# Two-layer attention and mixture-of-experts kernel: expert stages flat over all tiles, routing weights by DMA instead of by matmul

## The chip, the cores and the metric

The kernel runs on one core of one Trainium2 chip. The metric is the device time of one execution in microseconds (us), lower is better; a kernel's time is the median of its runs. A profiled execution also leaves a trace of every instruction.

## The reference, cut to what matters

Two layers run over 2048 tokens of width 128 (two sequences of 1024). Each layer is normalise, attention, gate, experts, and adds its result to the tokens. Layer 0 has 32 experts of inner width 64 and a shared one of 128; layer 1 has 16 experts of inner width 176 and a shared one of 352. Each token uses 4 experts, with weights from the gate; all experts are computed for all tokens, and the weight is zero where an expert was not chosen.

```python
cw = jnp.zeros((T, E), xf.dtype).at[jnp.arange(T)[:, None], indices].add(weights)
def body(y, p):
    w1e, b1e, w3e, b3e, w2e, b2e, we = p
    h = jax.nn.silu(xf @ w1e + b1e) * (xf @ w3e + b3e)
    return (y + we[:, None] * (h @ w2e + b2e), None)
y, _ = jax.lax.scan(body, y0, (w1, b1, w3, b3, w2, b2, cw.T))
z = jax.nn.silu(xf @ sw1 + sb1) * (xf @ sw3 + sb3) @ sw2 + sb2
return (y + z).reshape(shape)
```

Layer 1 has no biases, and the output projection of its attention is added to the same sum.

## The kernel before

**Stages.** `two_layers` runs six blocks one after the other: `prepare`, attention and `experts` for layer 0 (k = 0), then the same three for layer 1 (k = 1).
**Routing weights.** At the end of an attention stage the gate's result `cw` [tokens, experts + 1] is transposed by TensorE (`weights_turned`, L192) into PSUM, ScalarE copies the high part (float32r) to rows 0.. of `cw_split` (`weights_hi`, L203), and VectorE writes the rest to rows 64.. (`weights_lo`, L211).

**Experts.** All experts of a layer lie side by side as hidden rows, cut in chunks of 128 rows: K = 17 chunks for layer 0 and K = 25 for layer 1 (the last has 96 rows). Tokens are cut in NC = 4 tiles of 512. Every factor of a product is split in a high and a low part, so a product is three float32r matmuls. For one chunk and one tile:

- TensorE `rise(c)`: three matmuls for g (L1165 to L1167), three for u (L1169 to L1171), one (L1172) that spreads the routing weights over the chunk's rows: the 0/1 matrix `sel` times `cw_split` into a PSUM bank `c_ps`. 
- ScalarE: gate = silu(g) (L1226), later hid_hi = rounded hid (L1232).
- VectorE: up = u * gate (L1296 with bias for k = 0, L1298 for k = 1), hid = c_ps * up (L1302).
- GpSimd: hid_lo = hid - hid_hi (L1251).
- TensorE `fall(c)`: waits for hid_hi and hid_lo, then three matmuls into the one bank `y_ps` (L1179 to L1181), which sums over the chunks of the tile.

Each of these matmuls has 512 columns, 10 in a chunk. TensorE's order in a tile is rise(0), rise(1), rise(2), fall(0), rise(3), fall(1) and so on, then fall(K-2), fall(K-1). The token tile is the body of a hardware loop (`Fori`) on every engine, so rise(0) of a tile comes after the last fall of the one before, and `y_ps` is free only when VectorE has copied it to `yT` (L1314 for k = 0, L1316 for k = 1). g, u and c_ps have two banks each, y one, and one (z) serves the end. For k = 0 two matmuls (L1193, L1194) start y with the b2 bias; for k = 1 three more per tile add the projection (L1185 to L1187), whose input VectorE normalises inside the tile, at chunks K-6 to K-3 (L1286 reciprocal, then L1287 to L1289).

**Weights.** Sync (SP) loads w1, w3, w2 and `sel` in groups of up to three chunks into a ring of two (L1110, L1113); ScalarE copies the high parts (`split_hi`, L1214, `sel` too), GpSimd writes the low parts (`split_lo`, L1146). Groups 0 and 1 are split ahead of the first tile; groups 2 and 3 ahead of the first two gates, and later ones at chunks 3, 6, 9 and so on of the first tile. From the second tile on there are no weight loads.

**Transposes.** `yT` is [features, tokens]. For k = 0 it is turned back to rows at the start of `prepare` of layer 1 (L292, L377), for k = 1 at the end of `experts` (L1207, L1322), all 16 blocks after the last tile, followed by the store of the output (L1126).

## Time and profile before

| | us |
|---|---|
| median of 3 runs | 1406.43 (1398.53 to 1409.87) |
| the profiled execution's own time | 1408.63 |
| its span, first to last instruction | 1406.8 |
| TensorE busy | 1181.4 (84%) |
| ScalarE, VectorE, GpSimd busy | 761.5, 719.5, 550.8 |

The span begins with `prepare` and the first attention (to 235 us); experts of layer 0 run from 236 to 444 us, the second `prepare` and attention from 444 to 1115, experts of layer 1 from 1115 to the end. In a timeline a row is one instruction: start, length, engine, line, operands, and in brackets how long its engine sat idle before it and who released it. Matmuls are pipelined: successive starts tell their pace, and the lengths overlap.

### The profile page before, as it was taken

What the parts mean: (1) busy time and instruction counts of PE and PEld (TensorE: products, weight loads), DVE (VectorE), ACT (ScalarE), POOL (GpSimd) and SP (SyncE); (2) the same over time, 40 slices, a digit from 0 to 9 for tenths busy, and PEclk for the clock granted to TensorE, in tenths of its full rate; (3) what the DMA queues carried; (4) which work ended last, traced back from release to release, by engine and by line L of the source; (5) the groups of instructions that cost most, each with busy time, mean ns of one, the idle gap of its engine ahead of it and who ended that gap; (6) DMA issues with size and microseconds to landing.
All of it is one profiled execution on the core that took longest, in us unless ns stands there. A gap on an engine that the chain in (4) does not pass through costs nothing. (4 is left out here: it accounts for less than half of the span.)

```text
span 1406.8 us, 23122 instructions
## 1 busy us (share of the span) xinstructions
PE 1181.4 (84%) x8332; PEld 727.0 (52%) x8332; DVE 719.5 (51%) x998; ACT 761.5 (54%) x1136; POOL 550.8 (39%) x725
## 2 busy tenths in 40 slices
PE   3599996789986622899999999999999378898897
PEld 3233332567764521455555555555554256677685
DVE  5122221345556520676666666666664036575656
ACT  1388885644442101475777777777775255344443
POOL 1255553745443010033333333333322367454554
PEclk9999998899997555597999999999999689999999
DMA  3311101300000273877788888788761241000001
GB/s 114 149 43 49 42 31 60 105 0 0 0 0 6 82 253 111 270 188 206 185 222 227 215 235 226 223 222 224 225 206 28 81 142 29 0 0 0 0 0 30
DMA packets 119933, 155.76 MB, mean 111 GB/s; under 512 B 27806, under 2 KB 110880, under 8 KB 119840
## 3 DMA queue, kind: packets, MB, share of 16 engines
q1 hardware_dynamic: 101280, 145.30, 33.1%
q0 software_dynamic: 18560, 9.23, 4.4%
q8 instruction: 57, 0.93, 0.3%
q14 instruction: 36, 0.29, 0.1%
HBM read 81.97 MB, written 72.34 MB: 110 GB/s over the span
## 5 line engine op out<-in xcount | busy, mean ns | idle before, releaser
L1009 DVE TENSOR_REDUCE a_part<-a_duo 128x2 f32<-128x1024 f32 x256 | 311.5, 1225 | 196.3 <-PE a_duo L873 195.0
L971 ACT ACTIVATE a_probs<-a_duo 128x1024 f32<-128x1024 f32 x256 | 261.8, 1023 | 105.1 <-PE a_duo L912 99.0
L1251 POOL TENSOR_TENSOR f_hid_lo<-f_hid,f_hid_hi 128x512 fp32r<-128x512 f32 (+1 forms) x168 | 216.8, 1292 | 202.3 <-ACT f_hid_hi L1232 202.3
L818 POOL DMA_DIRECT2D scr_y1c<-a_y x256 | 132.0, 524 | 320.8 <-DVE a_y L1000 319.6
L967 ACT ACTIVATE a_rel<-a_rel_ps 128x384 f32<-128x384 f32 x256 | 126.0, 492 | 135.4 <-PE a_rel_ps L855 114.8
L623 ACT ACTIVATE a_probs<-a_duo 128x1024 f32<-128x1024 f32 x192 | 147.8, 813 | 36.0 <-PE a_duo L581 34.5
L927 PE MATMUL a_acc_ps<-a_probs,a_v 128*32 128x256 f32 x2048 | 166.9, 398 | 0.3 <-issue 0.2
L855 PE MATMUL a_rel_ps<-a_emb_all,a_q 24*128 24x384 f32 x256 | 121.0, 473 | 53.8 <-DMA a_kb<-scr_kb 31.0
L855 PEld LDWEIGHTS a_rel_ps<-a_emb_all,a_q 24*128 24x128 f32 x256 | 50.2, 196 | 161.6 <-issue 97.5
L570 POOL TENSOR_TENSOR a_probs<-a_probs,const 128x256 f32<-128x256 f32 x128 | 95.2, 763 | 86.7 <-ACT a_probs L623 86.7
L1226 ACT ACTIVATE f_gate<-f_g 128x512 f32<-128x512 f32 (+1 forms) x100 | 59.7, 597 | 121.0 <-PE f_g L1167 120.8
L1302 DVE TENSOR_TENSOR f_hid<-f_c,f_up 128x512 f32<-128x512 f32 (+1 forms) x168 | 116.1, 691 | 8.5 <-POOL f_hid_lo L1251 2.9
L1298 DVE TENSOR_TENSOR f_up<-f_u,f_gate 128x512 f32<-128x512 f32 (+1 forms) x100 | 68.8, 688 | 100.8 <-PE f_c L1172 84.1
L1232 ACT ACTIVATE f_hid_hi<-f_hid 128x512 fp32r<-128x512 f32 (+1 forms) x168 | 104.7, 623 | 24.5 <-DVE f_hid L1302 24.5
L601 PE MATMUL a_acc<-a_probs,a_v 128*32 128x256 f32 (+1 forms) x1280 | 116.3, 379 | 0.1
L912 PE MATMUL a_duo<-const,a_rel_raw 128*128 128x128 f32 x704 | 114.5, 290 | 0.0
L900 PE MATMUL a_duo<-a_q,a_ka 25*128 25x512 f32 (+3 forms) x416 | 104.0, 404 | 2.0 <-DMA a_q<-a_rows 0.7
L1165 PE MATMUL f_g<-x_hi,f_w_hi 128*128 (+1 forms) x168 | 69.4, 413 | 37.7 <-ACTq L1236 21.1
L581 PE MATMUL a_duo<-a_q,a_k 24*128 24x512 f32 (+3 forms) x384 | 86.3, 449 | 16.4 <-DMA a_k<-scr_k 15.1
L873 PE MATMUL a_duo<-a_ka,a_q 24*128 24x512 f32 (+3 forms) x416 | 99.1, 444 | 0.7 <-DVE a_rows L1020 0.7
L1179 PE MATMUL f_y<-f_hid_hi,f_w_hi 128*128 128x512 f32 (+1 forms) x168 | 69.7, 415 | 33.9 <-POOL f_hid_lo L1251 33.9
L912 PEld LDWEIGHTS a_duo<-const,a_rel_raw 128*128 128x128 f32 x704 | 75.8, 143 | 36.9 <-issue 30.5
(199 smaller groups left out, 2032.8 us busy)
## 6 DMA issues: line engine op xcount, KB each, us to landing
scr_rel<-a_rel SPq DMA_DIRECT2D x128, 384.0 KB, 3.9
a_rel_raw<-scr_rel SPq DMA_DIRECT2D x128, 384.0 KB, 4.3
f_raw<-in_w SPq DMA_DIRECT2D x33, 192.0 KB, 2.7
scr_q<-q_hi SPq DMA_DIRECT2D x4, 1024.0 KB, 7.9
scr_y1c<-a_y POOLq DMA_DIRECT2D x256, 8.0 KB, 3.4
a_q<-scr_q SPq DMA_DIRECT2D x40, 96.0 KB
a_k<-scr_k SPq DMA_DIRECT2D x32, 96.0 KB
a_q<-scr_q POOLq DMA_DIRECT2D x24, 96.0 KB, 5.4
```

The lines of the kernel that those rows point to most:

```text
L601: ins = pe.matmul(acc[h % 2][to:to + 32, lo:QUARTER], vs[:, pair % 2, hd, kt, :], probs[:, n % KEPT, hd, c * QUARTER + lo:(c + 1) * QUARTE ...
L623: act.activation(probs[:, n % KEPT, :, lo:HALF], duo[n % 3][:, :, lo:HALF], ACT.Sigmoid, scale=SCALE).then_inc(sig_done, 1)
L818: pool.dma_start(scr["y1c"][w, b, head, :, at:at + QUARTER], ys[32 * (2 * hd + c) + HD * w:32 * (2 * hd + c) + HD * (w + 1), h % 2, :]).th ...
L855: pe.matmul(rel_ps[:, 0:BAND], qs[to, home(pair), j * P:(j + 1) * P], emb_all[to, :], start=True, stop=True).then_inc(rel_ready, 1)
L912: ins = pe.matmul(out[:, at:at + P], rel_raw[:, (8 * pair + j) % RING, hd, c:c + P], ident, is_transpose=True, start=False, stop=True, ski ...
L927: ins = pe.matmul(acc[to:to + 32, 0:QUARTER], vs[:, pair % 2, hd, kt, :], probs[:, n % 4, at:at + QUARTER], start=(n % 8 == 0), stop=(n % ...
L967: act.activation(rel_sb[:, e % 4, r % 2, :], rel_ps[:, 0:BAND], ACT.Copy).then_inc(saved_act, 1)
L971: act.activation(probs[:, n % 4, :], bank_pair("t", n)[:], ACT.Exp, scale=SCALE).then_inc(exp_done, 1)
L1009: dve.tensor_reduce(part[:, h % 2, x, :, j % 4], bank_pair("s", m)[:].rearrange("p (h t) -> p h t", h=2), AX.X, ALU.max, negate=True).then ...
L1232: act.activation(hid_hi[0:m, c_ % 4, :], hid[0:m, c_ % 2, :], ACT.Copy).then_inc(hi_ready, 1)
L1251: pool.tensor_tensor(hid_lo[0:m, c % 4, :], hid[0:m, c % 2, :], f32(hid_hi[0:m, c % 4, :]), ALU.subtract).then_inc(lo_ready, 1)
L1302: dve.tensor_tensor(hid[0:m, c % 2, :], w, up[0:m, c % 2, :], ALU.mult).then_inc(hid_ready, 1)
```

## The change

1. *Routing weights by DMA.* `cw_split`, `sel`, its loads and copies, and the matmul L1172 go. ScalarE copies the transposed weights to one tile `cwT`; SP stores it to HBM (`scr["cw"]`) at the end of the attention stage and waits for the landing. In the expert stage SP reads, for each chunk and tile, the row of each expert that owns hidden rows of the chunk, broadcast over those partitions, into `share`, a ring of WB = 4. A chunk has one or two owners: 33 such DMAs per tile for k = 0 and 39 for k = 1, 288 in all, of 256 KB per chunk. `share_out(n)` waits for `hid_ready` n - 3.
2. *u in place.* u has three banks; VectorE writes up over u in PSUM, and hid = u * share.
3. *Flat.* One unrolled sequence over n = tile * K + chunk, 68 and 100 chunks, on every engine; no loop. rise(n) comes before fall(n-2) across tiles too. y has two banks. VectorE takes y of a tile out at chunk 3 of the next (`finish`).
4. *fall* waits for hid_hi, issues its first two matmuls, and only then waits for hid_lo.
5. *Turn inside.* TensorE transposes a finished tile at chunk 5 of the next into z, VectorE adds it to x at chunk 7 (`residual`), in both layers; `prepare` of layer 1 loses its transposes. The last tile is turned at the end of the stage.
6. *Bias.* b2 isn't split any more: one plain float32 matmul per tile, `b2` times `cwT`, ahead of the tile's first fall.
7. SP's order: loads 0 and 1, shares 0 to 3, the attention result (1 MB for k = 0, moved from ahead of the loads; 2 MB for k = 1), then in chunk order the other loads (each waits for `raw_lo`) and shares. The layer 1 normalisation of the projection's input moves from chunks K-6.. to K-8...

```diff
+def weights_stored(router, sb, scr, sp):
+    sp.wait_ge(router.cw_saved, NC)
+    sp.dma_start(scr["cw"][0:E + 1, :], sb["cwT"][0:E + 1, :]).then_inc(router.cw_stored, 16)
+    sp.wait_ge(router.cw_stored, 16)
...
 # SP
+            def share_out(n):
+                ti, c = n // K, n % K
+                wait(sp, hid_ready, n - WB + 1)
+                for e, a, b in owners(c):
+                    row = scr["cw"][e:e + 1, ti * CH:(ti + 1) * CH]
+                    sp.dma_start(share[a:b, n % WB, :], bass.AP(row.tensor, row.offset, [[0, b - a], [1, CH]])).then_inc(share_loaded[n % WB], 16)
...
+            for n in range(WB):
+                share_out(n)
...
+            for n in range(M):
+                if n in starts[:-3]:
+                    load(starts.index(n) + 2)
+                if n >= WB:
+                    share_out(n)
...
 # TensorE
-                    pe.wait_ge(gate_ready, ti * K + max(c - 1, 0) + 1)
-                    pe.wait_ge(hid_ready, ti * K + max(c - 1, 0) + 1)
-                    pe.matmul(w, sel[:, ch], sb["cw_split"][:, cols], start=True, stop=True).then_inc(u_ready, 1)
+                wait(pe, gate_ready, n - 1)
+                wait(pe, hid_ready, n - 2)
...
+                if c == 0:
+                    wait(pe, y_ready, ti - 1)
+                    if k == 0:
+                        pe.matmul(y, b2[0:E + 1, :], sb["cwT"][0:E + 1, cols], start=True, stop=False)
+                pe.wait_ge(hi_ready, n + 1)
+                pe.matmul(y, w_hi[2][0:m, ch], hid_hi[0:m, n % 4, :], start=(k == 1 and c == 0), stop=False)
+                pe.matmul(y, w_lo[2][0:m, ch], hid_hi[0:m, n % 4, :], start=False, stop=False)
+                pe.wait_ge(lo_ready, n + 1)
+                ins = pe.matmul(y, w_hi[2][0:m, ch], hid_lo[0:m, n % 4, :], start=False, stop=(k == 0 and c == K - 1))
...
+            for n in range(M + 2):
+                if n < M:
+                    rise(n)
+                if n >= 2:
+                    fall(n - 2)
+                if n >= K + 5 and n < M and (n - 5) % K == 0:
+                    turn((n - 5) // K - 1)
+            turn(NC - 1)
...
 # VectorE
+            for n in range(M):
+                dve.wait_ge(u_ready, n + 1)
+                dve.wait_ge(gate_ready, n + 1)
...
+                    dve.tensor_tensor(u, u, g, ALU.mult).then_inc(up_ready, 1)
+                dve.wait_ge(share_loaded[n % WB], 16 * shares(n))
+                wait(dve, lo_ready, n - 1)
+                dve.wait_ge(up_ready, n + 1)
+                dve.tensor_tensor(hid[0:m, n % 2, :], u, w, ALU.mult).then_inc(hid_ready, 1)
+                if k == 1 and K - 8 <= c < K - 4:
+                    quotient(ti, c - (K - 8))
+                if ti and c == 3:
+                    finish(ti - 1)
+                if ti and c == 7:
+                    residual(ti - 1)
+            finish(NC - 1)
+            residual(NC - 1)
```

## Rows read from the trace of the kernel before

**Rows 1.** Stretches: length; PE, PEld, DVE, ACT, POOL busy; clock, DMA share, GB/s.

```profile
1122.00:1142.00 20.00, 14.49 (x33) 9.78 (x34) 4.18 (x7) 11.16 (x24) 10.44 (x12) 0.60 0.62 214
...
1345.00:1385.00 40.00, 40.00 (x178) 33.12 (x177) 25.43 (x35) 19.51 (x36) 22.87 (x18) 1.00 0.00 0
```

**Rows 2.** Timeline of one steady chunk, experts of layer 1, first tile.

```profile
1185.79 0.39 PE L1172 MATMUL f_c<-cw_split,f_sel 128*128 x1
...
1188.07 0.62 ACT L1232 ACTIVATE f_hid_hi<-f_hid 128x512 fp32r<-128x512 f32 x1
1188.29 0.39 PE L1179 MATMUL f_y<-f_hid_hi,f_w_hi 128*128 128x512 f32 x1
...
1188.77 1.29 POOL L1251 TENSOR_TENSOR f_hid_lo<-f_hid,f_hid_hi 128x512 fp32r<-128x512 f32 x1 [0.86 <-ACT f_hid_hi L1232]
...
1190.55 0.39 PE L1179 MATMUL f_y<-f_hid_hi,f_w_hi 128*128 128x512 f32 x1
```

**Rows 3.** Timeline of the end of that tile: reciprocal, last chunks, next tile's start.

```profile
1187.64 3.34 DVE L1286 RECIPROCAL v<-v  x1
...
1194.42 0.47 PE L1179 MATMUL f_y<-f_hid_hi,f_w_hi 128*128 128x512 f32 x1 [0.92 <-POOL f_hid_lo L1251]
...
1197.95 0.39 PE L1167 MATMUL f_g<-x_lo,f_w_hi 128*96 x1
...
1202.96 0.69 PE L1179 MATMUL f_y<-f_hid_hi,f_w_hi 96*128 96x512 f32 x1 [1.04 <-POOL f_hid_lo L1251]
...
1206.84 0.79 PE L1165 MATMUL f_g<-x_hi,f_w_hi 128*128 x1 [1.06 <-DVE yT L1316]
```

**Rows 4.** Timeline: last g of the first tile, layer 0; its last two; layer 1's last.

```profile
297.26 0.39 PE L1167 MATMUL f_g<-x_lo,f_w_hi 128*128 x1
...
434.18 0.39 PE L1167 MATMUL f_g<-x_lo,f_w_hi 128*128 x1
...
436.48 0.39 PE L1167 MATMUL f_g<-x_lo,f_w_hi 128*128 x1
...
1393.29 0.39 PE L1167 MATMUL f_g<-x_lo,f_w_hi 128*96 x1
```

**Rows 5.** Timeline around the starts of both expert stages.

```profile
232.34 2.03 ACT L203 ACTIVATE cw_split<-a_duo 33x512 fp32r<-33x512 f32 x4 [2.21 <-PE a_duo L192]
...
235.73 0.37 SPq L1093 DMA_DIRECT2D f_b<-in_b  x1
...
236.63 1.65 SPq L1095 DMA_DIRECT2D f_b<-in_b  x1
...
252.49 1.35 ACT L1214 ACTIVATE f_w_hi<-f_raw 128x384 fp32r<-128x384 f32 x3 [4.53 <-DMA f_raw<-in_sel]
...
255.56 0.69 ACT L1226 ACTIVATE f_gate<-f_g,f_b 128x512 f32<-128x512 f32 x1
...
1132.57 0.60 ACT L1226 ACTIVATE f_gate<-f_g 128x512 f32<-128x512 f32 x1
```

**Rows 6.** DMA issues: tile, queue, count, KB each, median us to landing.

```profile
f_raw<-in_w SPq DMA_DIRECT2D x33, 192.0 KB, 2.7
...
scr_k<-x_hi SPq DMA_DIRECT2D x2, 1024.0 KB, 5.2
...
sgv<-in_bv SPq DMA_DIRECT2D x1, 64.0 KB, 3.5
```

**Rows 7.** Groups by line: busy us, mean ns, idle before; GpSimd's low parts of weights.

```profile
L1146 POOL TENSOR_TENSOR f_w_lo<-f_raw,f_w_hi 128x384 fp32r<-128x384 f32 (+4 forms) x51 | 42.6, 865 | 43.8 <-ACT f_sel L1214 43.8
```

**Rows 8.** Timeline: float32 matmuls; transposes, adds at the stages' ends; prepare's first sum.

```profile
448.47 2.29 DVE L380 TENSOR_REDUCE stat<-x 128x16 f32<-128x2048 f32 x1
...
1097.05 1.82 PE L927 MATMUL a_acc_ps<-a_probs,a_v 128*32 128x256 f32 x24
...
1400.18 0.60 PE L1207 MATMUL f_g<-const,yT 128*128 128x128 f32 x4
...
1402.74 0.68 DVE L1322 TENSOR_TENSOR x<-f_g,x 128x512 f32<-128x512 f32 x1
```

**Rows 9.** Waits of SP's queue: who waited for whom, us, times, longest.

```profile
SPq L786 <- DMA scr_y1c<-a_y: 23.2, 1, 23.2
```

More of the change, by code:

```diff
@@ L1088, in pieces, with owners, shares @@
             return [p for p in parts if p[2] > p[1]]
+        def owners(c):
+            r, end, out = c * P, c * P + CK[c], []
+            while r < end:
+                e = min(r // INTER, E)
+                to = min((e + 1) * INTER, end) if e < E else end
+                out.append((e, r - c * P, to - c * P))
+                r = to
+            return out
+        def shares(n):
+            return sum(len(owners(i % K)) for i in range(n % WB, n + 1, WB))
+        block = ctx.enter_context(nc.Block())
         @block.sync
@@ L1135, in split_hi @@
             eng.wait_ge(raw_loaded[n % 2], 16 * raw_count(n))
[L1136 removed]
+            for m in range(3):
                 for rows, a, b in pieces(m, c0, c1):
[L1138 removed]
+                    ins = copy(w_hi[m][0:rows, a:b], raw[0:rows, n % 2, m, a - c0 * P:b - c0 * P])
             ins.then_inc(raw_hi, 1)
@@ L1243, in _ @@
         @block.gpsimd
         def _(pool):
-            def token_tile(ti, first=False):
-                for c in range(K):
-                    if first and c in starts[:-3]:
-                        split_lo(pool, starts.index(c) + 2)
-                    m = CK[c]
-                    pool.wait_ge(hi_ready, ti * K + c + 1)
-                    pool.tensor_tensor(hid_lo[0:m, c % 4, :], hid[0:m, c % 2, :], f32(hid_hi[0:m, c % 4, :]), ALU.subtract).then_inc(lo_ready, 1)
             split_lo(pool, 0)
@@ L1254, in _ @@
             split_lo(pool, 1)
-            token_tile(0, first=True)
-            with pool.Fori(1, NC) as ti:
-                token_tile(ti)
+            for n in range(M):
+                m = CK[n % K]
+                if n in starts[:-3]:
+                    split_lo(pool, starts.index(n) + 2)
+                pool.wait_ge(hi_ready, n + 1)
+                pool.tensor_tensor(hid_lo[0:m, n % 4, :], hid[0:m, n % 2, :], f32(hid_hi[0:m, n % 4, :]), ALU.subtract).then_inc(lo_ready, 1)
         @block.vector
```

277 lines of the change are left out of this document (109 added, 168 removed).

## The prediction, as it went on record before the changed kernel was timed

> **What bounds the kernel now.** I read the page's 40 slices first, to find the two expert stages, and then the busy times of stretches. In a steady part of layer 1's experts TensorE is busy 40.00 of 40.00 us at full granted clock, every other engine under two thirds of that, and DMA idle [rows 1]. So inside a tile the stage goes at the pace of matmuls. Next the timeline of one chunk: the first y matmuls of two chunks start 2.26 us apart, ten matmuls, 0.226 each; for layer 0 two chunks are 2.30 apart, 0.230 each [rows 2, 4]. The reader should also see the chain beside it: from the start of the last matmul of rise (L1172, 1185.79) to the end of hid_lo (1188.77 + 1.29 = 1190.06) are 4.27 us, and the y matmul that needs it starts at 1190.55, 0.49 later, of which some 0.14 is the wake-up. So about 0.35 us of slack [rows 2].
>
> Then the end of a tile. Each of the last two falls waits 1 us for hid_lo, with no rise left to cover it; the granted clock falls to half (the y matmul takes 0.69 instead of 0.47), and the next rise waits 1.06 us for VectorE's copy of y and runs cold [rows 3]. The price of all this comes from the last g of tile 0 and of tile 3: 436.48 - 297.26 = 139.2 us for 51 chunks of layer 0, against 51 x 2.30 = 117.3; and 1393.29 - 1197.95 = 195.3 for 75 chunks of layer 1, against 169.5 [rows 3, 4]. So 22 and 26 us are lost at tile changes (and, in layer 1, to the reciprocal).
>
> **The change part by part.**
>
> *Tiles 1 to 3 of layer 0.* A chunk has nine matmuls: 51 x 9 x 0.230 = 105.6. Tile changes cost no idle time: rise(n+2) of the next tile covers the last falls, the second y bank takes away the wait for the copy, and `finish` comes after chunk 3, `turn` after the fall that follows it, so neither is waited for. Without an idle gap the clock has no reason to fall. Three turns of four transposes, 0.60 each [rows 8], are 1.8. Three float32 b2 matmuls aren't in the trace: from below four transposes of the same 512 columns, 0.60 with overlap, from above 24 matmuls of 256 columns, four side by side, in 1.82, so 0.61 for 512 [rows 8]; I take 0.6 each, 1.8. Together 109.2: **30.0 saved**. The Trainium skill (FP8 and Floating Point Precision, on true FP32) says such a matmul makes 4 passes; with it b2 would cost 4 x 0.23 = 0.92, and the sum would be 1 us less.
>
> Does the chain keep up? Counted in matmuls, the time from the end of rise to the y matmul that needs hid_lo is 3 + 7 + 3 + 7 + 1 = 21 before, and 3 + 6 + 3 + 6 + 3 = 21 after, because the wait for hid_lo moved behind two matmuls. The slack stays near 0.35. What VectorE writes to PSUM instead of SBUF has no row; it can cost nothing, or up to what PSUM reads cost. ScalarE's hid_hi (1188.07) waits for its own gate before it, so some 0.4 of extra in VectorE lies hidden. VectorE itself is busy 25.4 of 40 us [rows 1]; with two small additions per tile it has room in 2.04 us. The share DMAs take SP two issues of about 0.45 us per chunk, behind the wait for hid(n-4); the ring leaves four chunks (8.2 us), less 1.7 for issues and hid, 6.4 us to land. 192 KB land in 2.7, a broadcast of 64 KB in 3.5 [rows 6], and 256 KB in 2.04 us are 128 GB/s, against 214 moved in a loaded stretch [rows 1]. Hidden.
>
> *Tiles 1 to 3 of layer 1.* 75 x 9 x 0.226 = 152.6; nine projection matmuls 2.0; three turns 1.8. VectorE's reciprocal (3.34) holds up hid: the y matmuls around it are 1194.42 - 1190.55 = 3.87 apart, 1.6 more than normal [rows 2, 3]. The shorter chunk makes VectorE later still; I take 2.0 per tile (between 1.4, a third u bank helping, and 2.6, four chunks at 0.23), 6.0. Sum 162.4: **32.9 saved**.
>
> *Start and tile 0, layer 0.* The store of `cwT` stands between the stages. ScalarE's copies end at 234.4, SP began at 235.73; new: + 0.4 issue + 3.3 landing + 0.3 barrier = 238.4, 2.7 later. Bounds: landing 2.7 or 5.2 [rows 6], an issue of 1.65 as the 33-row b2 load [rows 5]; 2.1 to 5.8. Then 1 MB of shares and the moved 1 MB load stand before weight group 2, which the first gate waits for since its split comes first in ScalarE's program: I take it 2.1 later than 252.49 (0.6 if only issue counts, 6 if both MB drain at 214 GB/s). The sel copy (a fourth beside the three in 1.35) is out, 0.45: first gate 1.7 late [rows 5]. From it to 297.26 are 15 chunks: 15 x 0.23 = 3.45 saved, 0.45 for the next sel copy, 0.9 for two cold y matmuls that don't wait for hid_lo; GpSimd's splits of three at 0.865 [rows 7] still hold up hid_lo, and since that stall is measured from a faster pace, 0.5 is given back: 4.3. **2.6 saved.**
>
> *Start and tile 0, layer 1.* SP sat 23.2 us in the wait for y1c's landing [rows 9]; the store of 17 rows goes into that wait: nothing. The Trainium skill (DMA: Bandwidth & Descriptors, on how many engines a DMA uses) says the count must divide the slowest dimension, so 17 rows go through one engine; 139 KB at a sixteenth of 214 GB/s would be 10 us, at worst 1 us beyond the cover. Shares add 1 MB, sel takes 0.38 away: 0.66 MB at 214 GB/s are 3.1, issue alone 0.8; I take 2.0, less 0.45, so the first gate (1132.57) is 1.5 late. 23 chunks x 0.226 = 5.2, + 1.35 as above, - 1.0 for six splits, + 0.2 as reciprocal and split now fall together: 5.8. **4.3 saved.**
>
> *End of layer 0.* The last y takes one matmul after hid_lo, not three; then four transposes at half clock 0.9, one add 0.7 and the barrier, against sixteen transposes and four adds in `prepare`, whose first sum began at 448.47 [rows 8]. With y out at 442.8 it begins at 444.8: **3.7 saved** (3.0 to 4.3).
>
> *End of layer 1.* 0.7 earlier to y, and one add rather than four; the last began at 1402.74 [rows 8]. **1.8 saved** (1.4 to 2.6).
>
> Sum: 30.0 + 32.9 + 2.6 + 4.3 + 3.7 + 1.8 = 75.3. From the profiled execution's 1408.6 this gives 1333.3; the median stands 2.2 lower, so **1331 us**.
>
> **Rivals.**
>
> *A, the pace doesn't fall.* If the chain through VectorE, ScalarE and GpSimd gets longer by more than its slack, TensorE waits for hid_lo in every chunk. A chain that is d too long costs d/3 per chunk (rise(n+3) follows fall(n)), so VectorE's in-place write must be over 1 us slower to eat the 0.23. For it: only 0.35 of slack [rows 2]. Against: ScalarE's order hides 0.4. If all of it is eaten, 164 chunks x 0.23 = 38 come back: 1369.
>
> *B, slower than before: the shares land late.* No row shows one 2 KB row read 64 or 128 times at once. If the landing takes over 6.4 us, each further microsecond costs 1/4 per chunk, 42 us in all. The gain is gone at a pace of 2.04 + 75.3/168 = 2.49, a landing of 4 x 2.49 - 1.7 = 8.3 us; at 10 us the time is 1331 + 3.6 x 42 = 1482. Against: the 64 KB broadcast (3.5) lands no later than loads around it [rows 6].
>
> *C, better.* The splits and reciprocals hide in the slack of three u banks and the start costs nothing: 6 + 4 + 3 less, 1318.
>
> *D, tile changes still idle* (a wait of `turn` or `finish` that I take for free isn't): half of the 48 us back, 1355.
>
> **How the numbers follow.** Forecast 0.72, within 1318 to 1345 by the bounds (start of either stage +7, reciprocals +-3, runs +-5). A 0.08, D 0.06, C 0.07, B 0.07. The range 1316 to 1358 takes in the forecast, C and D and leaves out A and B, under 2 in 10. A measurement tells about 1% from no change. Faster by over 1% holds all but B: 0.92; within 1% 0.02; slower 0.06.
>
> **What would show it.** After: y matmuls of neighbouring chunks 2.04 to 2.07 apart; no half clock between the first tile and the last chunk of a stage; last g of tile 0 to that of tile 3 in 109 and 162 us; VectorE waits for u, not for a share DMA; SP's first DMA of layer 0's experts 3 to 8 us after the end of ScalarE's last copy; the first gates 1 to 3 us later than before relative to their stages' starts. I am wrong if hid waits for `share_loaded`, if fall waits for hid_lo in every chunk, or if g's first matmul of a tile still waits.

## The result, and the profile after

The changed kernel takes 1350.05 us, the median of four runs (1344.59 to 1356.12); the kernel before, on the same chips, takes 1402.48 (four runs, 1398.06 to 1409.87). The ratio is 0.962, 95% interval 0.958 to 0.967: faster, by 52 us. Of all runs here two lie over 1.5% above the fastest of their kernel (1432.18 us of the kernel before, 1359.93 us of experiment 4), and they stand outside the ratios. The forecast was 1331, its range 1316 to 1358. So the direction and the range held. But 1350 lies outside the 1318 to 1345 that the forecast gave its own case; the range reached beyond that only to take in rival D (the tile changes still idle). The sum did not hold: it promised 75.3 us, and the two profiled executions differ by 1408.63 - 1356.12 = 52.5. Where the missing 22.8 us are is the question of the rest.

To find them I cut both profiled executions at the same events. The cuts use the start of ScalarE's gate of a chunk, of which no record is missing. Times are in us; "SP first" is SyncE's first DMA of an expert stage, and gate n is the gate of the stage's chunk n. Both columns of stretches come from the timelines; those of before agree with [rows 4, 5 and 8].

| from ... to | before | after | won | forecast |
|---|---|---|---|---|
| start to last copy of y, attention 1 | 231.79 | 230.72 | 1.1 | 0 |
| to SP first, layer 0 | 3.94 | 5.70 | -1.8 | -2.7 |
| to gate 0 | 19.83 | 20.86 | -1.0 | 1.0 |
| to gate 16 (end of tile 0) | 42.13 | 40.11 | 2.0 | 4.3 |
| to gate 67 (tiles 1 to 3) | 139.22 | 111.16 | 28.1 | 30.0 |
| to the first sum of the preparation | 11.56 | 8.02 | 3.5 | 3.7 |
| to the first copy of y, attention 2 | 161.98 | 170.47 | **-8.5** | 0 |
| to the last copy of y | 488.49 | 490.02 | -1.5 | 0 |
| to SP first, layer 1 | 15.96 | 19.89 | **-3.9** | 0 |
| to gate 0 | 17.67 | 22.91 | **-5.2** | -1.5 |
| to gate 24 (end of tile 0) | 65.81 | 60.51 | 5.3 | 5.8 |
| to gate 99 (tiles 1 to 3) | 195.34 | 162.94 | 32.4 | 32.9 |
| to the end | 13.08 | 10.99 | 2.1 | 1.8 |

The two large terms came within 2 us. The loss is in places where the forecast had put nothing or little: the start of the second attention (no code differs there), the way from its last y to the experts of layer 1, and the first gates.

In the timeline of the changed kernel (start, duration, engine, line) a steady chunk of layer 0 looks like this, a y matmul with hid_lo, the three of g, the three of u, the next y:

```profile
342.89 0.39 PE L1192 MATMUL f_y<-f_hid_lo,f_w_hi 128*128 128x512 f32 x1
343.12 0.39 PE L1170 MATMUL f_g<-x_hi,f_w_hi 128*128 128x512 f32 x1
...
344.27 0.39 PE L1176 MATMUL f_u<-x_lo,f_w_hi 128*128 128x512 f32 x1
344.50 0.39 PE L1189 MATMUL f_y<-f_hid_hi,f_w_hi 128*128 128x512 f32 x1
344.73 0.40 PE L1190 MATMUL f_y<-f_hid_hi,f_w_lo 128*128 128x512 f32 x1
344.97 0.39 PE L1192 MATMUL f_y<-f_hid_lo,f_w_hi 128*128 128x512 f32 x1
```

Nine matmuls in 344.97 - 342.89 = 2.08 us, where there were ten in 2.30, and no bracket: nothing is waited for. Rival A (the pace does not fall) is out. So is B (shares land late). The page gives a share copy 3.0 and 3.2 us to land (medians), about half of the ring's 6.4; of all 288 copies one took longer than that, 7.4 us, at the start of layer 1's experts. In the group of VectorE's second product the largest releaser of its 29.9 us of idle time is GpSimd, and no share copy is among the releasers:

```profile
L1310 DVE TENSOR_TENSOR f_hid<-f_u,f_share 128x512 f32<-128x512 f32 (+1 forms) x168 | 116.2, 692 | 29.9 <-POOL f_hid_lo L1250 8.0
...
f_share<-scr_cw SPq DMA_DIRECT2D x144, 128.0 KB, 3.0
f_share<-scr_cw SPq DMA_DIRECT2D x44, 256.0 KB, 3.2
```

At a tile change of layer 0 TensorE has the b2 matmul besides (the profile records it as two), and here the gates are 3.33 us apart instead of 2.08:

```profile
303.89 0.39 PE L1176 MATMUL f_u<-x_lo,f_w_hi 128*128 128x512 f32 x1
304.21 1.12 PE L1187 MATMUL f_y<-cwT,f_b 33*128 33x512 f32 x2
305.27 0.50 PE L1189 MATMUL f_y<-f_hid_hi,f_w_hi 128*128 128x512 f32 x1
```

The experts of layer 1 start like this (SyncE's queue, then ScalarE; the bracket is the idle time before, and what ended it):

```profile
1079.62 0.26 SPq L207 DMA_DIRECT2D scr_cw<-cwT  x1
1096.95 0.37 SPq L1096 DMA_DIRECT2D f_wp<-in_wproj  x1
...
1100.58 2.81 SPq L1117 DMA_DIRECT2D f_share<-scr_cw  x6
1103.44 0.43 SPq L1127 DMA_DIRECT2D xn<-scr_y1c  x1
1103.91 0.91 SPq L1127 DMA_DIRECT2D v<-scr_y1c  x1
1104.87 2.62 SPq L1110 DMA_DIRECT2D f_raw<-in_w  x2
...
1117.20 1.35 ACT L1220 ACTIVATE f_w_hi<-f_raw 128x384 fp32r<-128x384 f32 x3 [13.64 <-DMA f_raw<-in_w]
1118.57 1.28 ACT L1234 ACT_TABLE_LOAD   x1
1119.86 0.60 ACT L1234 ACTIVATE f_gate<-f_g 128x512 f32<-128x512 f32 x1
```

Three things are to be seen. The store of the weights is issued at 1079.62, and the stage begins 17.3 us later. Weight group 2, issued from 1104.87, lands at 1117.20, behind 2 MB of the attention's y. And the gate stands behind the split of that group. Behind the store SyncE waits for its landing and that of y1c. The waits of its queue have both under one line, and after it the end of the stage (waited for; us, times, longest):

```profile
SPq L640 <- PEq L640: 9.7, 1, 9.7
SPq L768 <- DMA scr_y1c<-a_y: 7.0, 1, 7.0
```

The 9.7 us are the same before and after. The 7.0 run from the issue of the store to 1086.9. What moves in them is a thin stream; two windows of it (length; PE, PEld, DVE, ACT, POOL busy; clock, DMA share, GB/s):

```profile
1084.00:1086.00 2.00, 0.00 (x0) 0.00 (x0) 0.00 (x0) 0.00 (x0) 0.00 (x0) 0.50 0.07 26
1086.00:1088.00 2.00, 0.00 (x0) 0.00 (x0) 0.00 (x0) 0.00 (x0) 0.00 (x0) 0.50 0.00 1
```

The last copies of y1c were issued by 1081.9. A share of 0.07 is what one busy engine of sixteen gives, and it lasts up to 1086.

### The profile page after: what moved, and what is told of

Same layout as the page of the kernel before. It is cut to its first block and busy times, and to the rows that moved or that the text cites. A ratio compares the mean times of both kernels' runs of the same rounds, so it can differ in the third digit from the quotient of the medians.

```text
span 1354.3 us, 22279 instructions
## 1 busy us (share of the span) xinstructions
PE 1136.6 (84%) x8164; PEld 691.5 (51%) x8164; DVE 711.8 (53%) x984; ACT 754.6 (56%) x1119; POOL 546.3 (40%) x723
## 5 line engine op out<-in xcount | busy, mean ns | idle before, releaser
L909 PE MATMUL a_acc_ps<-a_probs,a_v 128*32 128x256 f32 x2048 | 170.0, 405 | 0.3 <-issue 0.2
L1310 DVE TENSOR_TENSOR f_hid<-f_u,f_share 128x512 f32<-128x512 f32 (+1 forms) x168 | 116.2, 692 | 29.9 <-POOL f_hid_lo L1250 8.0
L1170 PE MATMUL f_g<-x_hi,f_w_hi 128*128 128x512 f32 (+1 forms) x168 | 68.5, 408 | 57.7 <-POOL f_w_lo L1157 34.1
L1306 DVE TENSOR_TENSOR f_u<-f_u,f_gate 128x512 f32<-128x512 f32 (+1 forms) x100 | 69.7, 697 | 67.2 <-PE f_u L1176 43.0
L563 PE MATMUL a_duo<-a_q,a_k 24*128 24x512 f32 (+3 forms) x384 | 86.3, 449 | 16.1 <-DMA a_k<-scr_k 14.8
L622 DVE COPY a_y<-a_acc 128x256 f32<-128x256 f32 x32 | 13.6, 424 | 149.5 <-issue 88.5
```

The costliest lines, as they stand in the source:

```text
L909: ins = pe.matmul(acc[to:to + 32, 0:QUARTER], vs[:, pair % 2, hd, kt, :], probs[:, n % 4, at:at + QUARTER], start=(n % 8 == 0), stop=(n % ...
L1310: dve.tensor_tensor(hid[0:m, n % 2, :], u, w, ALU.mult).then_inc(hid_ready, 1)
```

## The experiments

All times of stretches are from profiles; medians and ratios are against the kernel before on the same chip. "Changed" stands for the changed kernel. Medians of one kernel differ by several us between chips and executions, so single terms are judged by stretches.

### 1. The changed kernel once more, and the start of the second attention

> The changed kernel, unchanged. Its profiled execution had TensorE at the lower clock for 133 us of the start of the second attention (468.6 to 601.7, until 185.1 us after the first sum of the preparation), the kernel before for 109 us (until 161.6 us after it), and the stretch up to the first copy of y took 8.5 us longer. Theory (chance of one execution, or of the point at which the clock comes back): the clock rises earlier this time, the stretch takes about 162 us instead of 170.5, and the execution 1347 or less. Rival (the changed kernel itself brings it, by what TensorE does or no longer does ahead of the attention): again about 170 us and a clock that rises 180 us or more after the first sum. Time: 0.962 of the kernel before by both.

Measured: 1354.79 us (1344.39 to 1361.92), 0.969 of before (0.963 to 0.976). The stretch to the first copy of y took 159.1 us instead of 170.5: the first theory. But the next stretch took 496.3 instead of 490.0, so the whole attention was 655.4 after 660.5 (650.5 before), and the execution was 1351.23, not 1347. Windows of TensorE at the start of this attention, the execution of above and then this one (length; PE, PEld, DVE, ACT, POOL busy; granted clock, DMA share, GB/s):

```profile
502.00:590.00 88.00, 61.02 (x267) 33.49 (x271) 33.51 (x41) 30.06 (x49) 2.23 (x4) 0.50 0.60 178
590.00:602.00 12.00, 11.16 (x105) 5.25 (x101) 7.65 (x9) 8.52 (x13) 3.62 (x8) 0.97 0.54 165
```

```profile
502.00:590.00 88.00, 63.10 (x377) 33.86 (x379) 41.77 (x51) 38.58 (x60) 6.73 (x13) 0.64 0.66 198
```

With the same program the clock is 0.50 through all 88 us in one execution and 0.64 on average in the other; in the same time TensorE issues 267 records in the one and 377 in the other. The eleven other profiles of this study, all with this attention unchanged, fill in the spread: from the first sum of the preparation to the last copy of y they took 651.2, 650.5, 658.4, 648.5, 647.6, 651.5, 661.0, 655.6, 649.0, 657.3 and 657.8 us (kernels 2 to 12 in their order). So one and the same program varies by 13 us there. What makes the clock return late in some executions is open.

That the 10.0 us which the profiled pair loses there are only chance is not shown. Without this attention the stretches of the pair add up to 62.5 us won, but the medians differ by 52.4, as the pair does. It is the same with the twelve kernels below: set against the kernel before on the same chip, their medians won 9.9 us less on average than their stretches outside this attention (19.0 less to 1.9 more; on one of the three chips nearly nothing is missing in three kernels of four). The kernel before left only one profile, of 1408.63 us, and its medians on the chips are 1398.71 to 1409.49. So either its other executions are shorter than the profiled one in this attention or in another stretch, or the change makes the attention longer; no run tells which.

### 2. The store of the weights in two DMAs

```diff
-    sp.dma_start(scr["cw"][0:E + 1, :], sb["cwT"][0:E + 1, :]).then_inc(router.cw_stored, 16)
-    sp.wait_ge(router.cw_stored, 16)
+    for a, b in ((0, E), (E, E + 1)):
+        sp.dma_start(scr["cw"][a:b, :], sb["cwT"][a:b, :]).then_inc(router.cw_stored, 16)
+    sp.wait_ge(router.cw_stored, 32)
```

> The store of the routing weights goes out as two DMAs, the experts' rows (32 in layer 0, 16 in layer 1) and the row of ones. Theory: in layer 1 the store of 17 rows is late because all of it goes through one DMA engine, and the expert stage waits for it. Then SyncE's first DMA of the expert stage of layer 1 comes 11 to 12 us after the last store of y, instead of 15.1, and the kernel is 3 to 4 us shorter (1346); in layer 0 nothing moves (33 rows, 5.7 us from the last copy of y). Rival (any store at this place costs that much, through its wait and landing): still 15 us, and no change in time.

Measured: 1348.92 us (1341.96 to 1350.33), 0.965 (0.962 to 0.968). SyncE's queue, and its wait behind the store:

```profile
1068.37 0.67 SPq L208 DMA_DIRECT2D scr_cw<-cwT  x2
1081.74 0.36 SPq L1097 DMA_DIRECT2D f_wp<-in_wproj  x1
...
SPq L769 <- DMA scr_y1c<-a_y: 2.7, 1, 2.7
```

The wait behind the issue is 2.7 us (7.0 in the changed kernel), and from the last copy of y to the stage it takes 15.93 us: 3.96 less than in the changed kernel, and the same as before (15.96). The store in layer 0, 33 rows, stays at 5.73. So 3.9 us of the loss are the shape of the 17-row store, and layer 0's store costs its 1.8 us by being there.

### 3. The attention's y behind weight groups 2 and 3

```diff
             for n in range(M):
                 if n in starts[:-3]:
                     load(starts.index(n) + 2)
+                if n == 1:
+                    ...  # the loads of yv, or of yv and ysum, that stood ahead of this loop
```

> The loads of the attention's y (1 MB in layer 0, 2 MB in layer 1) are issued behind the loads of weight groups 2 and 3 instead of ahead of them, and layer 0's wait for it moves from the start of VectorE's stream to the first sum of y. Theory: group 2 lands late because it stands behind these megabytes (in layer 1 issued from 1104.87, landed 1117.20), and the first gate stands behind its split. Then group 2 lands some 3 to 5 us after its issue, the first gate comes 12 to 14 us after the stage's first DMA in layer 1 (22.9 now) and 14 to 17 in layer 0 (20.9 now), and the kernel is 10 to 14 us shorter (1336 to 1340). Rival (the copies for the routing weights' shares and the issues on SyncE set it, or what is won at the gate is waited away at chunk 3 and at the fourth share): the first gate moves but the 25th g doesn't, and the time falls by less than 3 us.

Measured: 1344.42 us (1337.76 to 1347.28), 0.963 (0.960 to 0.965); the profiled execution 1337.76 after 1356.12, of which 10 us are attention 2. Gate 0 comes 17.7 us after SP first in layer 1 (22.9) and 17.5 in layer 0 (20.9): 5.2 and 3.4 us earlier, and 4.6 and 3.4 of it are kept to the end of tile 0 (gate 24 at 78.8 after 83.4, gate 16 at 57.6 after 61.0). The mechanism is right, the size in layer 1 is half: group 2 still landed 8.6 us after its issue.

```profile
1087.01 2.81 SPq L1117 DMA_DIRECT2D f_share<-scr_cw  x6
1089.86 0.91 SPq L1110 DMA_DIRECT2D f_raw<-in_w  x2
1090.81 1.25 SPq L1107 DMA_DIRECT2D f_raw<-in_w  x1
...
1098.49 1.35 ACT L1221 ACTIVATE f_w_hi<-f_raw 128x384 fp32r<-128x384 f32 x3 [8.41 <-DMA f_raw<-in_w]
```

Six share copies of up to 256 KB still stand ahead of it. The 5.2 us are more than the whole excess over the forecast in layer 1 (5.24 - 1.5 = 3.7).

### 4. b2 left out

```diff
-                        pe.matmul(y, b2[0:E + 1, :], sb["cwT"][0:E + 1, cols], start=True, stop=False)
...
-                pe.matmul(y, w_hi[2][0:m, ch], hid_hi[0:m, n % 4, :], start=(k == 1 and c == 0), stop=False)
+                pe.matmul(y, w_hi[2][0:m, ch], hid_hi[0:m, n % 4, :], start=(c == 0), stop=False)
```

> The matmul of b2 with the routing weights, which opens each y in layer 0, is left out, and with it the output's share of b2. Theory (the price that the trace of the changed kernel shows): each of tile changes 1 to 3 falls from 3.33 us to 2.08, 1.25 us each, and the kernel is 4 to 5 us shorter. Rival (the price of the forecast, 0.6 us, the rest of the interval being a wait of that chunk): the tile change falls to 2.7 only, 2 us in all.

Measured: 1347.33 us (1337.75 to 1359.93), 0.960 (0.955 to 0.965). The gates of tiles 1 to 3 are 107.42 us apart, 3.74 less, 1.25 per tile change; the interval of each change is 2.08 instead of 3.33. In tile 0 it gave 1.35. So the float32 matmul of 33 rows by 512 columns costs 1.25 us at full clock, twice the forecast's 0.6 and 5.4 float32r matmuls of 0.23.

### 5. Shares 1 to 3 behind weight group 2 too

On top of 2 and 3; SyncE's order is now groups 0 and 1, share 0, group 2, shares 1 to 3, group 3, the attention's y.

> On top of the split store of the routing weights and of the later loads of the attention's y: the copies of shares 1 to 3 are issued behind weight group 2, so that the order at the start of an expert stage is groups 0 and 1, share 0, group 2, shares 1 to 3, group 3, the attention's y. Theory (group 2 lands 4 to 5 us after its issue, and what is issued ahead of it sets the first gate): in layer 1 its issue moves from 6.4 us after the stage's first DMA to 5.5, in layer 0 from 9.1 to 5 or 6, and it no longer shares the engines with the shares' 0.4 to 0.6 MB: first gate at 12 to 14 us after the stage's first DMA in both layers (17.5 and 17.7 with the later loads alone). With the 4 us of the store the kernel is 10 us shorter than with the later loads alone (1334). Rival (the landing is set by the weights' own 0.6 MB and the issues, not by the shares): first gate stays at 17 or more, and only the 4 us of the store come.

Measured: 1332.26 us (1328.91 to 1335.43), 0.946 (0.939 to 0.953). Gate 0 comes at 13.1 us (layer 1) and 13.9 (layer 0), as the theory had it. But gate 24 comes 79.1 us after SP first, 78.8 in experiment 3: in layer 1 the gain is given back at once, in layer 0 two of four us stay. ScalarE shows where:

```profile
1087.82 0.60 ACT L1238 ACTIVATE f_gate<-f_g 128x512 f32<-128x512 f32 x1
1091.96 1.35 ACT L1224 ACTIVATE f_w_hi<-f_raw 128x384 fp32r<-128x384 f32 x3 [3.54 <-DMA f_raw<-in_w]
1093.21 0.58 ACT L1238 ACTIVATE f_gate<-f_g 128x512 f32<-128x512 f32 x1
...
1099.33 1.35 ACT L1224 ACTIVATE f_w_hi<-f_raw 128x384 fp32r<-128x384 f32 x3 [3.28 <-DMA f_raw<-in_w]
1100.59 0.58 ACT L1238 ACTIVATE f_gate<-f_g 128x512 f32<-128x512 f32 x1
```

The second gate waits behind the split of group 3, the fourth behind that of group 4. Neither group is needed by then; they only come first in ScalarE's program, and their loads share the queue with the attention's y.

### 6 and 7. One matmul less, and one more, per chunk

```diff
-                pe.matmul(u, w_lo[1][:, ch], sb["x_hi"][:, cols], start=False, stop=False)
```

> The changed kernel with one product less, w_lo times x_hi of u, which is left out of the output: 8 matmuls per chunk. Theory (TensorE's matmuls alone set the pace, 0.23 us each, and the other engines have room: VectorE's two products take some 1.6 us with the gaps, GpSimd's 1.3): 1.85 us per chunk in layer 0 and 1.82 in layer 1; gate 16 to gate 67 takes 99.4 us (111.2 now), gate 24 to gate 99 some 146 (162.9 now), the kernel 36 us less. Rival (the chain through gate, products and split is by now as long as the slots allow, so that it is the next bound at once): the pace stays above 1.95, and the two stretches fall by less than half of that.

```diff
+                pe.matmul(u, w_lo[1][:, ch], sb["x_lo"][:, cols], start=False, stop=False)
```

> The changed kernel with one product more in u, w_lo times x_lo, 10 matmuls per chunk as in the kernel before; everything else of the change stays. Theory (the sel matmul was worth one slot of 0.23 us per chunk, and the rest of the gain is the tile change): 2.31 us per chunk in layer 0, gate 16 to gate 67 takes 122.9 us (111.2 now, 139.2 before), gate 24 to gate 99 some 180 (162.9 now, 195.3 before), the kernel 38 us more. Rival (in-place u and shares from DRAM give something of their own, or the added matmul hides in a wait): less than 9 us and less than 13 us in the two stretches.

Measured (two executions each): with eight 1329.90 us (0.944, 0.935 to 0.952), with ten 1373.97 us (0.975, 0.966 to 0.984). With ten, tiles 1 to 3 of layer 0 took 122.72 us, forecast 122.9: the sel matmul was worth 11.6 of the 28.1 won there. In layer 1 it was 177.69, not 180.2, because part of the added work hides under the reciprocal (its interval is 3.15, and was 3.39). With eight, the pace does not get to 1.85 but alternates between 1.85 and 2.02, 1.93 on average; 103.17 and 155.08 us: two thirds of the theory's step in layer 0, under half in layer 1. Waits of TensorE in 20 us of its steady part in layer 0 (engine, line, waited for; us, times, longest):

```profile
PEld f_y L1191 <- POOL f_hid_lo L1249: 2.0, 8, 0.3
```

In eight chunks of ten TensorE waits up to 0.3 us for hid_lo. The chain through gate, products and splits is the next bound at 1.93. By the forecast's count, as an estimate, the chain to the y matmul has 19 matmuls to run beside here and 21 in the changed kernel, 0.46 us less; what TensorE loses is 3 x 0.08 = 0.25. So the slack was about 0.2, where I had read 0.35.

### 8 and 9. The tile change put back, in two steps

Rises held until the last fall of the tile before, as in the kernel before; ScalarE's last split of hid ahead of the next tile's first gate:

```diff
-            for n in range(M + 2):
-                if n < M:
-                    rise(n)
-                if n >= 2:
-                    fall(n - 2)
+            for ti in range(NC):
+                for c in range(K + 2):
+                    if c < K:
+                        rise(ti * K + c)
+                    if c >= 2:
+                        fall(ti * K + c - 2)
...
```

> The changed kernel with the rises of a token tile held back until the last fall of the tile before (TensorE), and the last split of hid of a tile ahead of the next tile's first gate (ScalarE): the pipeline drains at each tile change, as in the kernel before, while y stays in two banks. Theory (the tile change was idle time of the drained chain gate, product, product, split, split: 0.7 + 0.7 + 0.7 + 0.6 + 1.3 us less the two falls that still run): each of the six changes costs 3 to 4.5 us more, gate 16 to gate 67 takes 120 to 125 us (111.2 now), gate 24 to gate 99 some 172 to 176 (162.9 now). Rival (the two banks of y brought it, since y had to be copied out ahead of the next b2): the stretches grow by less than 1.5 us per change.

and on top of it one bank of y:

```diff
             for ti in range(NC):
+                wait(pe, y_ready, ti)
                 for c in range(K + 2):
...
-                if ti and c == 3:
-                    finish(ti - 1)
+                if c == K - 1:
+                    finish(ti)
```

> The drained kernel (rises held back until the last fall of the tile before) with y in one bank too: TensorE waits for the copy of y out of PSUM ahead of the next tile's first rise, VectorE copies it at the end of the tile, as in the kernel before. What then still differs from the kernel before at a tile change is its loop over the tiles with registers (and b2 in float32). In the kernel before the change of tile costs 7.5 us over four steady chunks in layer 0, in the changed kernel 1.25, in the drained one 3.4. Theory (the copy of y and its signals stand alone on the path): 1.5 to 2.5 us more per change than in the drained kernel, gate 16 to gate 67 takes 122 to 125 us (117.6 drained), and 2 to 3 us per change are left for the loop itself. Rival (the second bank gave nothing, the loop the rest): the stretch stays below 119. Rival (the bank is all of it): 128 or more.

Measured (two executions each): drained 1372.50 us (0.974, 0.965 to 0.982), with one bank 1374.97 us (0.982, 0.977 to 0.987). Tiles 1 to 3 of layer 0 took 111.16, 117.64 and 126.75 us: 2.2 per change for the drained pipeline (I had 3 to 4.5) and 3.0 for the bank (1.5 to 2.5). In layer 1 it was 162.94, 173.13 and 174.76. The first change of the one-bank kernel:

```profile
298.38 0.49 PE L1191 MATMUL f_y<-f_hid_lo,f_w_hi 128*128 128x512 f32 x1 [0.63 <-POOL f_hid_lo L1256]
...
300.20 0.50 PE L1191 MATMUL f_y<-f_hid_lo,f_w_hi 128*128 128x512 f32 x1 [0.62 <-POOL f_hid_lo L1256]
...
301.48 0.79 PE L1170 MATMUL f_g<-x_hi,f_w_hi 128*128 128x512 f32 x1 [0.79 <-DVE yT L1271]
```

These are the three waits that the kernel before has at the end of its tile. The second and third of them stand in [rows 3] (1202.96 and 1206.84), the first is this one:

```profile
1200.99 0.47 PE L1179 MATMUL f_y<-f_hid_hi,f_w_hi 128*128 128x512 f32 x1 [1.03 <-POOL f_hid_lo L1251]
```

The first two are 0.6 instead of 1.0 us because hid_lo is waited for two matmuls later. The 28.1 us of layer 0's tiles add up, if the parts don't change each other: sel 11.6, pipeline across the change 6.5, second bank 9.1; b2 in float32 instead of two float32r matmuls takes 3 x (1.25 - 0.46) = 2.4 back, the turns 3 x 0.45 = 1.4. What is left is 28.1 - 27.2 + 3.8 = 4.7 us, 1.6 per change: this much the loop over the tiles with its registers, or what else differs, cost. I had expected 2 to 3; by itself it wasn't tried.

Why the bank is worth 9.1 us in layer 0 and 1.6 in layer 1 is in the granted clock. Windows over one tile change each, from the last gate of a tile to gate 3 of the next: layer 0 and layer 1 with one bank, and the second change of layer 1 in the drained kernel (columns as above):

```profile
337.60:353.20 15.60, 13.58 (x39) 8.79 (x39) 6.82 (x10) 5.03 (x9) 5.65 (x5) 0.78 0.26 79
1248.10:1261.00 12.90, 10.42 (x42) 6.92 (x41) 6.27 (x10) 4.73 (x9) 5.51 (x5) 1.00 0.24 74
1245.30:1258.60 13.30, 11.61 (x41) 8.09 (x40) 5.58 (x9) 4.69 (x8) 5.42 (x5) 0.87 0.26 76
```

With one bank the clock falls at each of the three changes of layer 0 (0.88, 0.78 and 0.88 on average, 14.4 to 15.6 us long) and stays at 1.00 in layer 1 (12.8 us long). In the drained kernel it stays at 1.00 where a change takes 11.7 to 11.8 us and falls only in this one long change, 1.5 us more. So at full clock the bank is worth 1.1 us per change (12.8 less 11.7), and the rest of layer 0's 3.0 goes with the fall of the clock.

### 10. Start and first tile reworked

On top of the split store: the gate of chunk 0 ahead of the split of group 2; the splits of later groups spread over three chunks, behind gate and split of hid; one of three subtractions per group on VectorE; the b2 products of tiles 0 and 1 while TensorE waits for weights; the attention's y at chunk 6. The core of it on ScalarE:

```diff
-                if n in starts[:-3]:
-                    split(starts.index(n) + 2)
                 if n < M:
                     ...  # gate of n, split of hid of n - 1
+                for g, m in slots.get(n, ()):
+                    split(g, (m,))
```

> Start of the expert stages reworked, on top of the split store: order on SyncE groups 0 and 1, share 0, group 2, shares 1 to 3, group 3, and the attention's y only at chunk 6; ScalarE runs the first gate ahead of the split of group 2 and spreads the later splits over three chunks, behind gate and split of hid; VectorE takes one of the three subtractions of each weight group from GpSimd; the b2 products of tiles 0 and 1 are issued while TensorE waits for weights. Theory (in-order ScalarE and GpSimd hold the gates and hid_lo behind splits of groups that are needed later): SyncE's first DMA to gate 16 takes 50 to 53 us in layer 0 (61.0 in the changed kernel, 55.5 with the order of issues alone), to gate 24 in layer 1 68 to 72 us (83.4, 79.1), gates in tile 0 come 2.1 us apart where groups are split (3.8 now), gate 16 to gate 67 is 1.2 us shorter (b2 of tile 1); in all 26 to 32 us under the changed kernel, 1318 to 1325. Rival (the lower clock at the start of the stage and the copies of shares set tile 0): gate 16 and gate 24 come less than 2 us earlier than with the order of issues alone, 1330 or more.

Measured: 1324.11 us (1319.44 to 1325.58), 0.946 (0.941 to 0.950). Gate 0 is at 9.3 us in layer 0 and at 7.4 in layer 1 (20.9 and 22.9 in the changed kernel), and tile 0's gates at the splits are 2.0 to 2.3 apart (3.8), so the in-order engines were the cause of that (which of the edits did most of it isn't separated). The reason is in the changed kernel's timeline, here at layer 0's last split, a group of two chunks with gates 3.0 apart; the three subtractions of a full group take 2.96 us instead of 2.14, and the gates are 3.8 apart:

```profile
284.41 2.14 POOL L1157 TENSOR_TENSOR f_w_lo<-f_raw,f_w_hi 128x256 fp32r<-128x256 f32 x3
...
286.51 2.53 POOL L1250 TENSOR_TENSOR f_hid_lo<-f_hid,f_hid_hi 128x512 fp32r<-128x512 f32 x2
...
287.84 0.50 PE L1192 MATMUL f_y<-f_hid_lo,f_w_hi 128*128 128x512 f32 x1 [0.69 <-POOL f_hid_lo L1250]
```

Gate 16 is at 52.9 us, within the 50 to 53 of the theory, but gate 24 at 76.5, 4.5 later than its 68 to 72, and in both layers one interval, from gate 7 to gate 8, is long: 7.1 us in layer 0 and 11.4 in layer 1. VectorE waits there for a share:

```profile
1094.23 0.49 SPq L1135 DMA_DIRECT2D xn<-scr_y1c  x1
1094.76 0.47 SPq L1135 DMA_DIRECT2D v<-scr_y1c  x1
1095.28 4.06 SPq L1119 DMA_DIRECT2D f_share<-scr_cw  x5
```

```profile
1107.21 0.69 DVE L1336 TENSOR_TENSOR f_hid<-f_u,f_share 128x512 f32<-128x512 f32 x1 [10.40 <-DMA f_share<-scr_cw]
```

This is rival B of the forecast, made by my own edit: copies that follow 2 MB in the queue did not land within the ring's time.

### 11 and 12. The attention's y by token tile, and the reciprocal in eight pieces

```diff
-                if n == 6:
-                    ...  # all of yv, or of yv and ysum
+                if n in att_at:
+                    ti, w = att_at[n]
+                    ...  # 512 columns of one of them, 256 KB; from chunk 7 on, at most one per chunk
```

> The kernel with the reworked start, with the attention's y no longer loaded as one or two megabytes at chunk 6 but by token tile, 256 KB per DMA, one DMA at a time from chunk 7 on; the b2 products of tiles 0 and 1 stand behind the third rise instead of ahead of the first. Theory (the gate of chunk 8 stood still for 7.1 us in layer 0 and 11.4 in layer 1 because the copies of its share lay behind those megabytes in the DMA queue): these two intervals fall to 2.1 to 3 us, SyncE's first DMA to gate 16 takes 47 to 49 us (52.9), to gate 24 in layer 1 66 to 69 us (76.5), and the kernel is 12 to 15 us shorter (1310). Rival (the issue of the share copies on SyncE, up to 7.5 us for seven of them, is late by itself): the stall spreads over the chunks from 8 on and less than half of it is won.

```diff
-                if part == 0:
-                    dve.reciprocal(ysum[:, cols], ysum[:, cols]).then_inc(quotient_step, 1)
+                if part < PARTS:
+                    some = slice(ti * CH + part * w, ti * CH + (part + 1) * w)   # w = 64
+                    dve.reciprocal(ysum[:, some], ysum[:, some]).then_inc(quotient_step, 1)
```

> The kernel before it (y by token tile), with the reciprocal of the attention's sums in eight pieces of 64 columns, one per chunk from chunk 10, instead of one of 512; product, copy and difference follow at chunks 18 to 20. Theory (3.3 us at a stretch is what VectorE cannot absorb, 0.4 us per chunk is: it is idle for 0.5 us of each): the interval of 3.39 us in tiles 1 to 3 of layer 1 falls to 2.1 to 2.3, that of 2.73 stays or moves, gate 24 to gate 99 takes 157 to 159 us (162.9), and the kernel is 4 to 6 us shorter. Rival (each added VectorE instruction delays hid by its own length, since products and gates are chained): 0.2 us or more per piece, 1.6 per tile, and nothing is won.

Measured: 1317.42 us (1314.99 to 1324.67), 0.940 (0.936 to 0.945), and 1318.30 us (1310.41 to 1324.96), 0.942 (0.937 to 0.946); 1310, and then 4 to 6 less, were expected. By token tile, gate 16 is at 47.9 us after SP first, as expected, and gate 24 at 73.6, where 66 to 69 was expected: the two long intervals are gone, but in layer 1 the intervals from chunk 9 to 22 are 2.04 to 4.0, and VectorE still waits 11.9 us in nine places of tile 0 for shares. So in layer 1 part of the stall only spread, as the rival had it.

In the stretch the reciprocal did what it should, and a little more. From gate 24 to gate 99 it takes 156.71 us instead of 162.95, 2.1 us per tile (157 was the theory's best). The intervals of 3.39 and 2.73 have both become 2.04; what is left above 2.1 are those with the projection (2.74) and with the turn (2.50). The pieces and their neighbours on VectorE:

```profile
1225.40 0.70 DVE L1339 TENSOR_TENSOR f_u<-f_u,f_gate 128x512 f32<-128x512 f32 x1
1226.23 0.69 DVE L1343 TENSOR_TENSOR f_hid<-f_u,f_share 128x512 f32<-128x512 f32 x1
1226.84 0.54 DVE L1322 RECIPROCAL v<-v 128x64 f32<-128x64 f32 x1
1227.44 0.70 DVE L1339 TENSOR_TENSOR f_u<-f_u,f_gate 128x512 f32<-128x512 f32 x1
```

From 1225.40 to 1227.44 are 2.04 us, of which VectorE is busy 1.9: eight pieces of 0.54 take 1.0 us more than the 3.34 in one, and cost nothing. The two medians don't show it: they are the same within their spread, and the single runs of each differ by 10 and 15 us. The second attention isn't the reason in the profiles (657.3 and 657.8 us). So the 6 us are shown by the stretch alone. Against the kernel before either stands at 0.94, where the changed one stood at 0.962 and 0.969.

## Why the prediction was right, and where its sum was wrong

*The pace and the tile changes: right.* Nine matmuls per chunk, 2.08 and 2.04 us, no wait in the steady chunk, and in tiles 1 to 3 28.1 and 32.4 us won against 30.0 and 32.9. Experiment 7 gives the sel matmul its 0.23 per chunk, 8 and 9 give the tile change its two parts. The reason that the forecast gave for the second part, that rise covers the falls and the second bank the copy, is what they show, with the bank the larger (9.1 against 6.5 us) in layer 0, where the clock falls without it. In layer 1, where it stays up, it is the other way round (1.6 against 10.2, of which 1.5 is one long change in the drained run).

*The total: in the range partly by luck.* The range held 1350 because it took in rival D, and D didn't come about: without b2 the intervals at a tile change are the steady 2.08 (experiment 4). What filled that part of the range are the terms below and the second attention.

*The slack: read too large.* It was 0.35 in the forecast, and by experiment 6 about 0.2. It was enough for nine matmuls.

*b2: the term was mis-sized.* The step was "from above 24 matmuls of 256 columns, four side by side"; I took 0.6, and it measured 1.25 (experiment 4). It is the 1.9 us missing in tiles 1 to 3. In tile 0 it was left out of the sum altogether, since before it stood ahead of the first g, and cost 1.35 there. The bound from above was none: its row has matmuls with weights of 128 rows by 32 columns, and nothing in the trace tied four of them side by side to one of full width. The Trainium skill's page on precision (FP8 and Floating Point Precision, TensorE Precision Notes) has four passes for true float32, which with 0.23 us each is an estimate of 0.92; the runs show more.

*Tile 0: gains that were not there.* In layer 0 it won 2.0 us, not 4.3. That is 16 x 0.23 = 3.7 for the matmuls, 1.35 back for b2, and 0.1 to 0.2 back for each of three splits. The 0.45 for the sel copy and the 0.9 for cold matmuls, two terms of the forecast, can't be seen. In layer 1 it won 5.3, not 5.8: an interval with a split takes 3.82 us and took 3.91, so 0.1 of its 0.23 is won, in each of the last four of six, where GpSimd's splits hold up hid_lo.

*The store in layer 1: the step failed.* "The store of 17 rows goes into that wait: nothing." It costs 3.9 us (experiment 2). The wait of 23.2 us [rows 9] was real, but the store can be issued only when ScalarE has copied the weights, 2.6 us behind the last copy of y, and y1c has landed 3.4 us after that (experiment 2: 0.7 of issue and 2.7 of wait). So 3.4 us cover the store and not 23, and it took 7.3 (0.3 of issue and 7.0 of wait). The Trainium skill (DMA: Bandwidth & Descriptors, Why a DMA increments its semaphore by 16 and not by 1) takes the largest number of engines up to 16 that divides the slowest dimension, so one for 17 rows. The trace agrees, with its DMA share of 0.07, and so does the gain of 3.96 us from 16 rows and one. The forecast had cited the rule, worked out 10 us, and set them against the wrong cover.

*The first gates: the term was mis-sized.* In layer 0, group 2 landed at 254.62, 2.1 us later than before, as forecast, and the first gate at 257.28, 1.7 later, as forecast; but the first attention ended 1.1 us earlier, which the forecast didn't have, so the start is 1.1 us longer than I said. In layer 1 it is 3.7 us more. I had taken 2.0 for the megabyte of shares ahead of group 2, by its size; but the attention's y, 2 MB, stands there as well, and a load of 192 KB lands only behind all 3 MB. In the kernel before it stood there too, and group 2 landed 14.6 us after the stage's first DMA. I took that for the price of a start. It was the price of the queue's order: experiment 3 has 5.2 us of it, 5 another 4.6.

*The second attention: outside the forecast.* The allowance for runs was 5 us either way; the same code varies by 13. Whether all of the pair's 10.0 us are such variation is open, since the medians lack them too (experiment 1).

*The shares: right.* Rival B stays without a trace in the changed kernel and appears in experiment 10, where 2 MB go ahead of them.

With the second attention taken out, the profiled pair won 62.5 us, and the 12.8 that are missing from 75.3 are: store 3.9, starts 1.1 and 3.7, tile 0 2.3 and 0.5, tiles 1 to 3 1.9 (b2) and 0.5, less 1.1 for the first attention and 0.1 at the ends.

## What to carry to other kernels

When one instruction per chunk is taken away on the engine that bounds, its price times the count was a good number (11.6 us of 11.7 in layer 0; 14.8 of 17.3 in layer 1, where part of it hides under the reciprocal), and the chain beside it tells how often that can be done again (here not even once in full). The starts of stages can't be priced like that: list the queue of DMAs and each in-order engine's program up to the first useful result, and ask of every entry ahead of it whether it is needed yet; the order of loads and splits was worth more here than any operation that was left (13 us at the start of layer 0 and 10 at that of layer 1 by experiment 11, with b2 moved and one subtraction given to VectorE). And split what an engine does at a stretch into pieces that fit about into its idle time per chunk, even where the pieces cost more together.

## What the runs showed of the hardware

- A float32 matmul of 33 rows by 512 columns takes 1.25 us at full clock, a float32r one 0.23.
- A store of 17 rows of 8 KB ran with a DMA share of 0.07, one engine of sixteen, for 6 to 7 us (26 GB/s); in 16 rows and one it landed within 2.7 us of the end of its issue.
- A DRAM row of 2 KB read up to 128 times at once, up to 256 KB, landed in 3.0 to 3.2 us (medians; 7.4 at most); behind 2 MB in the queue VectorE waited over 10 us for it.
- An issue on SyncE took 0.45 us in most rows and 1.3 behind much data: the issues of two loads of 192 KB took 2.62 us behind 3 MB in the changed kernel and 0.91 without the 2 MB of them in experiment 3.
- A reciprocal of 64 columns takes 0.54 us, of 512 columns 3.34.
- In the kernel with one bank of y the granted clock fell at layer 0's tile changes (0.78 to 0.88 on average over 14.4 to 15.6 us) and stayed at 1.00 at layer 1's.
- The same attention took from 647.6 to 661.0 us, with TensorE's clock at its lower level for longer in the profiled execution of the changed kernel.
